# TensorE's attention loop written out step by step, one buffer per token block, and the first token block loaded one step earlier

## What is computed

```python
x = L0_attn_hidden_states                                # (1, 2048, 1024)
h = _layernorm(x)
q, k, v = (h @ w.T + b for w, b in ...)                  # each reshaped to (B, S, 32 heads, 32)
scores = jnp.einsum('bshd,bstd->bsht', q, k) / np.sqrt(32)
context = jnp.einsum('bsht,bstd->bshd', jax.nn.softmax(scores, axis=-1), v)
x = x + context.reshape(B, S, E)
y = _layernorm(x)
gate, up = y @ dq1.T, y @ dq2.T                          # dq1, dq2, dq3: w1, w2, w3 rounded to a 16-level
x = x + (jax.nn.silu(gate) * up) @ dq3.T                 # code in blocks of 64 (NF4), hidden width 2752
```

## Time and profile before

| | us |
|---|---|
| median of 3 runs | 1922.84 (1922.05 to 1928.06) |
| the profiled execution, its own time | 1925.85 |
| its span in the trace | 1924.1 |
| busy TensorE / VectorE / ScalarE / GpSimd | 1843.8 / 1726.5 / 1377.9 / 1252.9 |
| steps 2 to 13, the loop (us 114.96 to 482.42) | 367.46 |
| the residual's load (`x_res`, 512 KB), median from issue to landing | 4.6 |

### The profile page before, as it was taken

One profiled execution on the slowest core, in us unless ns is written; L12 is line 12 of the kernel. 1 busy time (PEld: TensorE's weight loads), 2 busy tenths in 40 slices (PEclk: granted clock), 3 DMA queues, 4 the chain that ended last, 5 costly groups with the idle time before them and its releaser, 6 DMA issues. The chain is left out here.

```text
span 1924.1 us, 42902 instructions
## 1 busy us (share of the span) xinstructions
PE 1843.8 (96%) x16470; PEld 889.9 (46%) x16470; DVE 1726.5 (90%) x1848; ACT 1377.9 (72%) x1523; POOL 1252.9 (65%) x706
## 2 busy tenths in 40 slices
PE   7898999989979999999999999999999999999998
PEld 6554454445434444444444444444444444444443
DVE  6798988879878999999999999999999999999985
ACT  7233332323247899898898998989989889899881
POOL 0133434343465787887977878778787797786961
PEclk9999999989989999999999999999999999999999
DMA  9445655555296332221121221122122122122114
GB/s 317 143 134 156 176 157 185 137 177 164 76 253 178 118 57 54 47 63 44 44 65 44 45 64 44 44 56 53 44 49 60 44 49 60 44 50 56 39 28 186
DMA packets 252931, 182.86 MB, mean 95 GB/s; under 512 B 177792, under 2 KB 220800, under 8 KB 252800
## 3 DMA queue, kind: packets, MB, share of 16 engines
q1 hardware_dynamic: 221600, 167.28, 31.3%
q10 hardware_dynamic: 31200, 13.64, 3.3%
HBM read 114.29 MB, written 24.12 MB: 72 GB/s over the span
## 5 line engine op out<-in xcount | busy, mean ns | idle before, releaser
L1717 DVE SCALAR_TENSOR_TENSOR bank<-signs,bank 128x1024 f32<-128x1024 int8 (+2 forms) x756 | 920.3, 1217 | 53.2 <-ACT signs L1583 25.8
L1878 PE MATMUL bank<-x2T,w12T 128*128 128x512 f16 x4128 | 896.5, 380 | 8.1 <-DMA x2T<-x_lo_dram 5.1
L1583 ACT ACTIVATE signs<-w_first,compare_bias 128x1024 int8<-128x1024 f32 (+1 forms) x588 | 630.6, 1138 | 9.9 <-PE bank L1066 8.3
L1878 PEld LDWEIGHTS bank<-x2T,w12T 128*128 128x128 f16 x4128 | 404.0, 98 | 497.0 <-DMA x2T<-x_lo_dram 5.6
L1583 ACT ACTIVATE signs<-w_last,compare_bias 128x1024 int8<-128x1024 f32 (+2 forms) x294 | 314.4, 1119 | 0.8 <-DVE w_first L1717 0.6
L1066 PE MATMUL bank<-wT,xT_hi 128*128 128x512 f16 x768 | 301.2, 392 | 2.4 <-PEq L321 2.4
L1066 PE MATMUL bank<-wT,xT_lo 128*128 128x512 f16 x768 | 300.2, 391 | 0.0
L1906 PE MATMUL bank<-w3T_hi,hT_hi 128*128 128x512 f16 x672 | 255.5, 380 | 6.5 <-DMA w3T_lo<-half 3.8
L1908 PE MATMUL bank<-w3T_hi,hT_lo 128*128 128x512 f16 x672 | 255.4, 380 | 0.0
L1907 PE MATMUL bank<-w3T_lo,hT_hi 128*128 128x512 f16 x672 | 255.3, 380 | 0.0
L1497 POOL TENSOR_TENSOR acc<-acc,hidden 128x512 f32<-128x512 f32 x160 | 201.1, 1274 | 27.4 <-ACT hidden L1624 26.6
(11 more groups left out here) (140 smaller groups left out, 2141.1 us busy)
## 6 DMA issues: line engine op xcount, KB each, us to landing
ff_raw<-in_L_ffn_w SPq DMA_DIRECT2D x63, 512.0 KB, 4.9
w_first<-in_L_ffn_w SPq DMA_DIRECT2D x41, 512.0 KB, 3.8
w_last<-in_L_ffn_w SPq DMA_DIRECT2D x19, 512.0 KB, 4.0
x_nat<-in_L_attn_hidden_states SPq DMA_DIRECT2D x16, 512.0 KB, 5.5
x_res<-in_L_attn_hidden_states SPq DMA_DIRECT2D x16, 512.0 KB, 4.6
x<-x_res SPq DMA_DIRECT2D x16, 512.0 KB, 3.8
acc<-x SPq DMA_DIRECT2D x4, 2048.0 KB, 8.8
out<-acc SPq DMA_DIRECT2D x15, 512.0 KB, 2.6
```

The costliest lines, as they stand in the source:

```text
L1583: nc.scalar.activation(signs[0:rows, ring(v, k), 0:cols], w_nat(v % SLOTS)[0:rows, 0:cols], ACT.Sign, scale=COMPARE[SUMMED[k]][0], bias=co ...
L1717: V.scalar_tensor_tensor(to, part, HALF_STEP[SUMMED[k]], total, ALU.mult, ALU.add).then_inc(sign_used, 1)
L1878: last = nc.tensor.matmul(dst, w, x[:, toks, c], start=c == 0 and i == 0, stop=c == C - 1 and i == 2)
```

## The change

TensorE's program uses `straight_steps` in place of `middle_steps`, so its 12 loop steps are written out. The `sem_inc(held)` instructions in its two attention parts go. The block tensor `x2T` becomes four tensors. Blocks 1 to 3 stay together over `wT`; block 0 lies behind `acc`, in memory that only buffers of the setup part used (`w_raw1`, `w_raw2` and their neighbours) and that no attention step uses. `load_tokens(0)` comes in the generator ahead of everything else and gets a `yield` of its own, and SyncE's step calls it at the end of step 14 (`ahead`), behind the residual's load.

```diff
@@ step in sync
                     sp.wait_ge(projected, 6 * n + 4)
                     next(feed)
+                if ahead:
+                    next(ahead)
@@ score_part, and the same in mix_part
-                    if t % HALF == 0:
-                        pe.sem_inc(held, 1)
@@ tensor
             def whole_program(step):
                 feed = feed_program(pe)
-                first_steps(step)
-                middle_steps(pe, step, feed)
-                tail(feed)
+                straight_steps(step, tail, feed)
                 for _ in feed:
                     pass
@@ feed_forward
         w_first = sb("w_first", [P, SLOTS - 1, E])
-        x2T = sb("x2T", [P, T, 2, C, P], F16)
+        x2T_later = [sb(f"x2T{b}", [P, ST_BLOCK, 2, C, P], F16) for b in range(1, SB)]
         w_last = sb("w_last", [P, E])
...
         acc = sb("acc", [P, T, E])
+        sb("apart", [P, 16])
+        x2T_first = sb("x2T0", [P, ST_BLOCK, 2, C, P], F16)
...
-        x2T_hi, x2T_lo = x2T[:, :, 0], x2T[:, :, 1]
+
+        def tokens_of(b, i):
+            return (x2T_first, *x2T_later)[b][:, :, i]
@@ sync of feed_forward (load_tokens, turn_tokens and gate_up address tokens_of in place of x2T)
             for slot in range(SLOTS):
                 sp.sem_inc(w_in[slot], 16)
+            load_tokens(0)
+            yield
             load(0, 3, P)
-            load_tokens(0)
             sp.wait_ge(x2_turned, 32 * (T - 3))
             turn_early(0)
             yield
```

More of the change, by code:

```diff
@@ L1395, in load_tokens @@
                 sp.wait_ge(x2_out, 32 * (b * ST_BLOCK + count + 1))
-                for part, dram in ((x2T_hi, x2_hi_dram), (x2T_lo, x2_lo_dram)):
-                    sp.dma_start(part[:, tiles].rearrange("p t c s -> p t (c s)"),
+                for i, dram in enumerate((x2_hi_dram, x2_lo_dram)):
+                    sp.dma_start(tokens_of(b, i)[:, 0:count].rearrange("p t c s -> p t (c s)"),
                                  dram.rearrange("(t p) f -> p t f", p=P)[:, tiles]).then_inc(x2_in[b], 16)
@@ L1409, in turn_tokens @@
                 sp.wait_ge(x2_hi_done, n + 1)
-                sp.dma_start_transpose(x2T_hi[:, n], x2_half[:]).then_inc(x2_turned, 16)
+                sp.dma_start_transpose(tokens_of(n // ST_BLOCK, 0)[:, n % ST_BLOCK], x2_half[:]).then_inc(x2_turned, 16)
                 sp.wait_ge(x2_lo_done, n + 1)
-                sp.dma_start_transpose(x2T_lo[:, n], x2_low).then_inc(x2_turned, 16)
+                sp.dma_start_transpose(tokens_of(n // ST_BLOCK, 1)[:, n % ST_BLOCK], x2_low).then_inc(x2_turned, 16)
             sp.sem_inc(w_ready, 64)
@@ L1849, in gate_up @@
                 tile, par = r * 2 + p, sb_ % 2
-                toks = slice(sb_ * ST_BLOCK, (sb_ + 1) * ST_BLOCK)
                 pe.wait_ge(x2_in[sb_], 32)
@@ L1875, in gate_up @@
                         hi, lo = w12T_hi[:, p, m, c, 0:outs], w12T_lo[:, p, m, c, 0:outs]
-                        passes = ((hi, x2T_hi), (hi, x2T_lo), (lo, x2T_hi))
+                        passes = ((hi, 0), (hi, 1), (lo, 0))
                         for i, (w, x) in enumerate(passes):
-                            last = nc.tensor.matmul(dst, w, x[:, toks, c], start=c == 0 and i == 0, stop=c == C - 1 and i == 2)
+                            last = nc.tensor.matmul(dst, w, tokens_of(sb_, x)[:, :, c], start=c == 0 and i == 0, stop=c == C - 1 and i == 2)
                             if c == C - 1 and i == 2:
```

## The result

The changed kernel takes 1894.32 us (median of 4 runs, 1892.80 to 1894.59), the one before 1924.45 us in the same comparison. The ratio is 0.984 (95% interval 0.9822 to 0.9859): 30 us faster, 1.6%. The forecast was 1888.4, the range 1878 to 1904.

A forecast was written before the change was run, and what follows sets the result against it. TensorE's loop back edges, then a chain through VectorE, were taken as the bound. Written-out loop 30.9 us, less 2 for stalls, plus 5.5 from the tail: 34.4 off the 1922.84 us median gives 1888.4 us, range 1878 to 1904.

The forecast's parts named there:

- Loop written out: TensorE's steps 2 to 13: all five back edges go, an iteration takes 56.1 us, 30.9 us gained.
- limit of 56.0 us: Two-step iteration: VectorE's work of 28.25 us plus the circle through VectorE of 27.74 us allow no less.
- The half clock: TensorE behind the five back edges: half of 29.35 us of work, 14.7 us, would not be there at 2.4 GHz.
- Stalls of written-out code: Late code blocks in TensorE's bursts, steps 4 to 13: 6 stalls, 5.6 us, of which 2 us count as lost.
- Rival D: Late code stalls all 40 bursts, with half clock: 77 us lost against 36.4 gained, 1963 us; 3%.
- `held`: Removing 64 increments handled only by TensorE's sequencer: 0 gained, with ends of 0 and 6 us.
- The moved load: Block 0's load at the end of SyncE's step 14, behind the residual load: cost 0.
- The tail: Step 15 and the feed-forward start: with block 0 loaded earlier, all engines move earlier, 5.5 us gained, ends 0 and 12.
- A: Attention steps run at TensorE's own 26.88 us: gain 44.9 us, with the tail 1872 to 1875 us; 4%.
- B: The single residual buffer's load lands 2 us later, 1.2 us a step lost over 12 steps: 1903 us; 13%.
- C: The early load only shifts the wait in the tail, which gives nothing: 1894 us; 13%.
- E: Nothing to see: written-out stalls cost what the back edges did, or VectorE hid the loop's slack; 3%.

The follow-up runs named there:

- Experiment 4: The kernel before with TensorE's loop as 3 iterations of 4 steps, two back edges in place of five; 1913.14 us, ratio 0.9945.
- experiment 5: The kernel after with semaphore increments padding each attention step, 111 in step 0, so block boundaries fall inside the first score burst; 1894.49 us, ratio 0.9837.
- experiment 9: The kernel after with block boundaries placed inside the bursts by padding only in steps 4 to 14; 1889.46 us, ratio 0.9817.
- 10: The kernel of experiment 9 with VectorE's first look of each step moved behind the normalisation; 1889.77 us, ratio 0.9823.
- 7: The kernel after with VectorE's first look of each step moved behind the normalisation of the next tokens; 1904.66 us, ratio 0.9901.
- 6: The kernel of experiment 5 with the padding counted so that a block is exactly the first mixing burst; 1900.05 us, ratio 0.9861.
- experiment 3: The kernel after with the 64 `held` semaphore increments put back; 1896.11 us, ratio 0.9851.
- experiment 2: The kernel after with the two-step hardware loop and the increments put back, leaving the token tensors and block 0's early load; 1919.1 us, ratio 0.9972.
- experiment 1: The kernel before with only TensorE's 12 loop steps written out, increments and the one token tensor kept; 1903.63 us, ratio 0.9894.
- experiment 8: The kernel after with token block 1's load moved ahead of the second pair of early transposes; 1894.35 us, ratio 0.9834.

## Why the prediction was right

**Size and base.** The sum said 34.4 us. The two profiled spans differ by 1924.1 - 1892.7 = 31.4. The forecast missed the median by 5.9 us: 3.0 of it in the sum, of which 2.5 are setup and step 0 (below), and the rest because the profiled execution before lies 3.0 us over the median it was set against, while that after lies only 0.3 over its own.

**Loop written out.** Forecast 30.9 less 2, so 28.9; measured 28.2. An iteration is 56.25 us at first, as the 56.1 taken, and 339.23 / 6 = 56.5 on the mean. Experiment 4 shows that it goes by the edge. The prediction's limit of 56.0 us isn't one: experiments 5, 9 and 10 have two-step stretches of 55.0 to 55.2 us. The half clock it put at 14.7 us, outside its sum, was 12.6. The next to be late is TensorE at its transposes, waiting for VectorE, in 8 of 12 steps with 0.4 to 1.0 us.

**Stalls of written-out code.** Forecast for steps 4 to 13: 6 stalls, 5.6 us. Measured: six (us 182.2, 218.7, 252.1, 289.7, 323.1, 388.7), which sum to 5.6, none with half clock. The agreement is luck, better than an estimate from 3 of 20 bursts deserves: experiments 5 to 7, with the same matmuls, have between 0.6 and 14.6 us of them in the loop. What the prediction called wandering is a rule, the block boundary. Rival D failed because a boundary alone costs nothing. A burst, 128 matmuls and as many weight loads, is as long as a block, so each burst has a boundary in it or at its end, in experiment 5 too, and there "issue" is 0.6 us in the whole loop. What counts is where it lies: over the ten traces with the loop written out, up to us 490, 35 of 47 bursts with the boundary 224 to 255 instructions behind their start have a stall, and 2 of 418 with it under 192.

The Trainium skill, "Runtime: NRT & Kernel Launch", section "Instruction fetch mechanics", calls such crossings mostly hidden. By that experiments 5 and 6 would take the same time; they differ by 12.4 us in the loop, so for these bursts of small matmuls the runs disagree.

**`held`.** Cost 0 forecast, and 0 within the measurement (experiment 3).

**The moved load.** Its own cost was set at 0. Step 14 is 1.5 us longer, but its extra stall, 1.81 us at us 459.7 with half clock to us 464.1, stands 20 us ahead of the load at 479.90. So the load didn't cause it. In experiment 2, where it is moved as well, step 14 takes 0.7 more, and in experiments 5, 6 and 9, with it moved and the boundaries placed, 0.4 less than before.

**The tail.** Forecast 5.5; steps 14, 15 and the opening give -1.5 + 7.8 - 0.7 = 5.6. Step 15 was put at 7.5 and gave 7.8, the wait for block 1 at 6.7 and was 5.91. VectorE's wait for the store of x1, which was to stay at 5.6, fell to 4.05. What the prediction didn't see is that loop and tail don't add. Experiments 1 and 2 give 20.0 and 4.5 us, 24.4 together, where the change gives 30 (by the medians' intervals that difference is barely told from none; the traces place it: experiment 1's opening takes 109.3 us, the change's 104.7). Its sum for the loop edit alone would have been 28.9, and experiment 1 has 20: the stall in mixing was a delay that hid the late block.

**The rivals.** A (steps of 26.88 us) fails on VectorE, busy for 53.58 us of a 56.25 us iteration; B on the loop's mean of 56.5 us where it had 58; C on step 15's 7.8 us; D and E on the time.

**Missed.** Setup and step 0, which the change doesn't touch, are 2.5 us longer. It doesn't belong to the change: experiment 8, the same as the kernel after in all of this part, has 88.68 us. Kernels without padding in step 0 range from 87.6 to 90.6 us. Of the 2.5 us, 1.7 stand ahead of the first projection matmul (us 64.70 and 66.36) and 0.9 in step 0, where TensorE's half-clock stretch is 6.83 us in the kernel after and 3.41 us in the kernel before. Why the setup varies isn't settled.

## What to carry to other kernels

A loop whose code is fetched anew on each turn costs at every turn (here 4.7 us of idle time and 2.9 us by the slow clock on TensorE, of which 5 to 6 us reached the loop's time), and writing it out is worth this much and no more than the next engine leaves. In written-out code, count the instructions: in this kernel, bursts of tiny matmuls emptied a 256-instruction block in 1.3 us, faster than the next arrived, and the block boundary should lie where the block before it takes longer to run. Padding to fix it was worth 4 to 5 us here. A delay that goes may have been hiding another: ask of every stall removed what its engine arrives at next, and keep megabytes of transfers away from bursts (2 MB issued just ahead of one lengthened its stall by 3.4 us).

## What the runs showed of the hardware

- **Stalls at block boundaries.** In the three programs that I counted, every "issue" stall of TensorE in written-out steps stood at the same place modulo 256 instructions, 0.3 to 3.6 us long, and ended 1.2 to 1.6 us after a packet of code had landed. At the five back edges of the kernel before that time is 1.8 to 2.0 us. In the kernel after, 10 of its packets arrive in two steps, and 2 x 1236 / 256 = 9.7. The attention loop of the kernel before runs 2496 TensorE instructions an iteration and brings 11 packets; the feed-forward loop runs 1188 and brings none at all in 600 us.
- **Code waits behind data.** The same instruction stalled for 0.68 us in the kernel after, where block 1's 2 MB are issued at us 524.04, and for 4.04 us where they are issued 4.5 us ahead of the burst (experiment 8), with a packet that starts 3.4 us later and takes as long. Likewise a pair of DMA transposes issues in 3.0 to 3.3 us, and in 9.0 to 9.7 behind 2 MB. That both wait for the same DMA engines is how I read it; no run takes them apart.
- **Increments on TensorE's queue.** 44 among 31 matmuls of 512 columns cost nothing that can be seen (experiment 9), 111 some 5 to 6 us (experiment 5, which differs from experiment 9 in nothing else up to step 1: 95.38 us against 90.62, and 30.05 against 24.34 from the first projection matmul on; the setup varies by 2 us between traces).
